# Second layer's edge stage: x1 rows formed in PSUM by identity products, one PSUM buffer for the sums

## The reference

```python
h = relu(layernorm(x))
# first layer: attention messages, summed by dst, then Wo
x = x + h + segment_sum(msg, dst) @ Wo.T + bo          # this is "x1" below
# second layer: weighted graph convolution and a two-layer MLP
h = relu(layernorm(x))
deg = segment_sum([edge_weight, ones], [src, nodes])
norm = rsqrt(deg)[row] * ew * rsqrt(deg)[col]           # edges and self loops
h7 = segment_sum((h @ W)[col] * norm, row) + b          # row = src, col = dst
x = x + relu(h7 @ W1 + b1) @ W2 + b2
```

## Time and profile before

| | |
|---|---|
| time, median of 3 runs | 1871.58 us (1869.59 to 1871.85) |
| the profiled execution | 1868.97 us, of which its span is 1867.3 us |
| busy share of the span | PE 87%, DVE 76%, ACT 60%, POOL 66% |
| first layer's edge stage with what precedes it | from 0 to about 690 us |
| second layer's edge stage | about 690 to 1045 us |
| node stage in full flow | from about 1097 us |

### The profile page before, as it was taken

How to read it: one execution, slowest core, us unless ns; L and a number is a source line. 1 busy time by engine, 2 the same in 40 slices (tenths; PEclk the granted TensorE clock), 3 DMA queues, 4 the chain that set the end, 5 groups by cost and what they waited for, 6 DMA issues and landing times.

```text
span 1867.3 us, 29386 instructions
## 1 busy us (share of the span) xinstructions
PE 1629.1 (87%) x6406; PEld 1099.9 (59%) x6406; DVE 1412.2 (76%) x5503; ACT 1119.3 (60%) x2092; POOL 1227.1 (66%) x864
## 2 busy tenths in 40 slices
PE   8788999999999967676675169999999999999998
PEld 4355666666666635454454046666666666666666
DVE  7986777777777639777776497888888888888873
ACT  0155555556666522222222378889889889989984
POOL 3246777777777646888887765666666666666650
PEclk9999999999999987878777679999999999999999
DMA  9997666666666655555556678999999999999981
GB/s 370 419 415 244 175 175 174 174 174 175 177 177 185 195 136 115 118 111 108 113 115 126 136 200 248 255 266 271 269 268 268 267 270 267 267 268 269 274 230 75
DMA packets 148023, 398.67 MB, mean 214 GB/s; under 512 B 20144, under 2 KB 56756, under 8 KB 147974
## 3 DMA queue, kind: packets, MB, share of 16 engines
q1 hardware_dynamic: 89830, 280.18, 43.8%
q0 software_dynamic: 56416, 115.46, 32.8%
q10 hardware_dynamic: 1728, 2.50, 0.4%
HBM read 217.84 MB, written 180.23 MB: 213 GB/s over the span
## 4 chain that ended last, share of the span: by engine, by line
PE 27%; POOL 25%; issue 13%; DMA 11%; DVE 10%; ACT 7%; another core or an unknown queue 4%; SPq 3%; ACTq 0%; DVEq 0%; POOLq 0%
POOL sums_dram L488 9%; DMA out_dram<-cg 8%; PE bank L1361 6%; PE bank L1350 6%; POOL kept L578 6%; PE bank L1246 4%; POOL cg L492 4%; POOL b_rs L484 4%; ACT z L1054 4%; DVE cg L958 3%; PE bank L1178 2%; PE bank L1253 2%; PE bank L1340 2%; SPq L394 1%
## 5 line engine op out<-in xcount | busy, mean ns | idle before, releaser
L1350 PE MATMUL bank<-kept,w 128*128 128x512 f32 x784 | 355.4, 596 | 0.0
L1361 PE MATMUL bank<-w_sb,kept 128*128 128x256 f32 x1568 | 354.3, 379 | 0.0
L578 POOL TENSOR_TENSOR kept<-kept 128x1024 f32<-128x1024 f32 x98 | 232.4, 2371 | 183.4 <-DVE cg L958 183.4
L1361 PEld LDWEIGHTS bank<-w_sb,kept 128*128 128x128 f32 x1568 | 297.9, 190 | 81.9 <-issue 46.4
L488 POOL DMA_INDIRECT sums_dram<-ub,sidx x148 | 244.1, 1649 | 91.3 <-issue 42.3
L1314 PE MATMUL bank<-cg,en 128*128 128x256 f32 x386 | 132.8, 489 | 124.7 <-issue 80.6
L484 POOL TENSOR_TENSOR b_rs<-b_ve,minus_half 128x8 f32<-128x8 f32 x102 | 210.5, 2064 | 28.7 <-DVE b_ve L975 28.7
L1350 PEld LDWEIGHTS bank<-kept,w 128*128 128x128 f32 x784 | 142.6, 192 | 142.3 <-issue 142.3
L1145 ACT ACTIVATE kept<-kept,b_nb,b_rs 128x256 f32<-128x256 f32 x392 | 202.2, 588 | 21.9 <-DVE b_nb L948 21.9
L1246 PE MATMUL bank<-qkv_w,zT 128*128 128x512 f32 x392 | 192.0, 612 | 21.4 <-DVE msg L815 18.0
L1135 ACT ACTIVATE kept<-kept,b_nb,b_rs 128x256 f32<-128x256 f32 x392 | 202.2, 589 | 12.5 <-DVE b_nb L948 12.5
(11 more groups left out here) (172 smaller groups left out, 3260.3 us busy)
## 6 DMA issues: line engine op xcount, KB each, us to landing
sums_dram<-cg SPq DMA_DIRECT2D x196, 512.0 KB
kept<-in_x_dram SPq DMA_DIRECT2D x97, 512.0 KB, 5.7
kept<-sums_dram POOLq DMA_DIRECT2D x97, 512.0 KB, 9.8
cg<-sums_dram SPq DMA_DIRECT2D x97, 512.0 KB, 8.7
out_dram<-cg SPq DMA_DIRECT2D x97, 512.0 KB, 9.8
row_d<-in_dst_dram SPq DMA_DIRECT2D x49, 128.0 KB
row_k<-keys_dram SPq DMA_DIRECT2D x24, 256.0 KB
row_s<-in_src_dram SPq DMA_DIRECT2D x24, 256.0 KB
```

The costliest lines, as they stand in the source:

```text
L578: pool.tensor_tensor(X1[k.slot(8)], X[k.slot(4)], H[k.slot(2)], ALU.add).then_inc(g_xh, 1)
L1350: ins = pe.matmul(bank[:, 2 + m, :], w01[:, c, m * P:(m + 1) * P], hT[k.slot(2)][:, c * GN:(c + 1) * GN], start=(c == 0), stop=(c == KC - 1))
L1361: ins = pe.matmul(to, rT[k.slot(2)][:, c * GN + j * P:c * GN + (j + 1) * P], w2_sb[:, c, :], start=False, stop=(c == KC - 1), skip_group_c ...
```

## The change

DVE no longer adds `C0` to `kept`. PE gets, between its lookups and its sums, a new step for quad `k = s`: for each pair of chunks an identity product of the two `kept` rows into one PSUM bank, and a second identity product of the gathered rows, accumulated onto it. Four products of 128x512 float32 per quad leave x1 in banks 0 and 1. PE waits for the gathers of quad s and, from the second quad on, for `n_h` of quad s - 1, since there is one such buffer. PE, not DVE, now increments `n_x1`. DVE's statistics and ACT's relus read the banks. The sums use banks 6 and 7 for every quad, and wait for the copy of the quad before rather than of the one before that.

```diff
 # VectorE
-                    dve.wait_ge(n_c0[q], a.turns(2, 16 * Q))
-                    dve.tensor_tensor(quad(kept, a, slice(None)), quad(kept, a, slice(None)), C0[q][:, 0:n, :],
-                                      ALU.add).then_inc(n_x1, 1)
                     dve.wait_ge(n_sel, a.value(1))
                     dve.tensor_tensor(quad(norm, a), quad(found, a), quad(ew_f, a), ALU.mult).then_inc(n_norm, 1)
-                    pass_on(dve, (n_x1, a.value(1)))
+                    dve.wait_ge(n_x1, a.value(1))
                     for i in range(n):
-                        ins = dve.bn_stats(st[q][:, i, :], kept[:, bass.ds(a.value(0, Q) + i, 1), :]
-                                           .rearrange("p a d -> p (a d)"))
+                        ins = dve.bn_stats(st[q][:, i, :], bank[:, i // 2, i % 2 * D:(i % 2 + 1) * D])
 # ScalarE
-                        ins = act.activation(H1e[q][:, i, :], kept[:, bass.ds(a.value(0, Q) + i, 1), :]
-                                             .rearrange("p a d -> p (a d)"), ACT.Relu, bias=nb[q][:, i, :],
-                                             scale=rs[q][:, i, :])
+                        ins = act.activation(H1e[q][:, i, :], bank[:, i // 2, i % 2 * D:(i % 2 + 1) * D], ACT.Relu,
+                                             bias=nb[q][:, i, :], scale=rs[q][:, i, :])
-                        ins = act.activation(UB2[q][i].rearrange("p i d -> p (i d)"), bank[:, 6 * q + i, :], ACT.Copy)
+                        ins = act.activation(UB2[q][i].rearrange("p i d -> p (i d)"), bank[:, 6 + i, :], ACT.Copy)
 # TensorE
+                if k.within(NQ):
+                    n = chunks(k)
+                        pe.wait_ge(n_c0[k.slot(2)], k.turns(2, 16 * Q))
+                    if k.past(1):
+                        pe.wait_ge(n_h, k.value(0))
+                    for i in range(n // 2):
+                        pe.matmul(bank[:, i, :], identity[:, :],
+                                  kept[:, bass.ds(k.value(0, Q) + 2 * i, 2), :].rearrange("p c d -> p (c d)"),
+                                  start=True, stop=False)
+                        ins = pe.matmul(bank[:, i, :], identity[:, :],
+                                        C0[k.slot(2)][:, 2 * i:2 * i + 2, :].rearrange("p c d -> p (c d)"),
+                                        start=False, stop=True)
+                    ins.then_inc(n_x1, 1)
                 if a.within(NQ):
                     q, n = a.slot(2), chunks(a)
                     pe.wait_ge(n_en, a.value(1))
                     pe.wait_ge(n_h, a.value(1))
-                    if a.past(2):
-                        pe.wait_ge(n_UB, a.value(-1))
+                    if a.past(1):
+                        pe.wait_ge(n_UB, a.value(0))
                     for to in range(n):
                         for i in range(to, n):
-                            ins = pe.matmul(bank[:, 6 * q + to // 2, (to % 2) * D:(to % 2 + 1) * D],
+                            ins = pe.matmul(bank[:, 6 + to // 2, (to % 2) * D:(to % 2 + 1) * D],
```

More of the change, by code:

```diff
@@ L880, in messages2 @@
                     ins.then_inc(n_cnt, 1)
-                    if a.reg is None and a.off == NQ - 1:
-                        dve.wait_ge(n_c0[q], 16 * Q * (a.off // 2) + 16 * n)
-                    else:
-                        dve.wait_ge(n_c0[q], a.turns(2, 16 * Q))
-                    dve.tensor_tensor(quad(kept, a, slice(None)), quad(kept, a, slice(None)), C0[q][:, 0:n, :],
-                                      ALU.add).then_inc(n_x1, 1)
                     dve.wait_ge(n_sel, a.value(1))
                     dve.tensor_tensor(quad(norm, a), quad(found, a), quad(ew_f, a), ALU.mult).then_inc(n_norm, 1)
-                    pass_on(dve, (n_x1, a.value(1)))
+                    dve.wait_ge(n_x1, a.value(1))
                     for i in range(n):
-                        ins = dve.bn_stats(st[q][:, i, :], kept[:, bass.ds(a.value(0, Q) + i, 1), :]
-                                           .rearrange("p a d -> p (a d)"))
+                        ins = dve.bn_stats(st[q][:, i, :], bank[:, i // 2, i % 2 * D:(i % 2 + 1) * D])
                     ins.then_inc(n_st, 1)
@@ L1305, in messages2 @@
                     ins.then_inc(n_look, 1)
+                if k.within(NQ):
+                    n = chunks(k)
+                    if k.reg is None and k.off == NQ - 1:
+                        pe.wait_ge(n_c0[k.slot(2)], 16 * Q * (k.off // 2) + 16 * n)
+                    else:
+                        pe.wait_ge(n_c0[k.slot(2)], k.turns(2, 16 * Q))
[9 more added lines that the diff above has]
+                    ins.then_inc(n_x1, 1)
                 if a.within(NQ):
```

## The result

The changed kernel takes 1882.27 us (median of 5 runs, 1878.30 to 1888.31), the kernel before 1871.58 us (5 runs, 1869.59 to 1872.37). The ratio is 1.007 with a 95% interval of 1.0052 to 1.0088: 10.7 us slower. The forecast was 1874, with a range of 1861 to 1891. The profiled execution took 1882.79 us, of which the span is 1881.2; the profiled pair is thus 13.9 us apart in span, the medians 10.7.

A forecast was written before the change was run, and what follows sets the result against it. POOL was taken to bound the edge stage. 20 rounds of 13.7 us against 279.0 give -5.0, start +7.5, tail +0.5, hence +3.0 on 1871.58: 1874.6, rounded to 1874, range 1861 to 1891.

The forecast's parts named there:

- What bounds: Edge stage before the change: POOL itself, with its scatters, gathers and issue gaps, is the bound; no engine releases it.
- 17 us of long scatters: Edge stage, 72 scatters: 129.7 us, against 112.3 at 1.56 each; some 17 of 253 us are standstill, mostly from the add.
- Part 1: Add leaves VectorE: POOL no longer stands still for it; POOL's own round 13.1 us, between 12.9 and 13.9.
- the brush of 0.1 to 0.3 us: POOL's second and third scatters of a round: likely slowed this much by VectorE's counting products, which move toward them.
- Rival 3: Edge rounds: the standstill only moves to the counting products; rounds 14.0 to 14.3 us, time 1879 to 1887; chance 0.16.
- Part 2: x1 on PE: 3.44 us at full clock, fully inside the loop from relus to relus, which becomes 12.9 us.
- Part 3: PE's clock in the edge rounds: a fall costs 1.8 us in full, giving 13.7 us a round; ends 13.1 and 14.9.
- one in three: PE's gaps in the edge rounds: one of three this size lowers the clock, adding 1.8 / 3 to 13.1 us.
- Both rivals of the clock: Edge rounds: clock holds, 12.9 to 13.3 us, chance 0.25; or falls at each gap, 14.5 to 14.9 us, chance 0.13.
- Part 4: Start, tail and rest: first scatter 7.5 us later (5.5 to 9), tail 0.5, the other changes nothing.
- The tail +0.5: Last quads: POOL waits for landings, not PE; the copy of the 24th sums up to 1 us late, so 0.5 us.
- slower, 0.41: Whole kernel: chance 0.41 of slower, against 0.27 faster and 0.32 same, where same is 1867.8 to 1875.3 us.

The follow-up runs named there:

- thin: Kernel before with the add cut to one of each chunk's 256 columns, the rest left out: 1835.3 us, ratio 0.9898.
- split add: Kernel before with the one add of 128x1024 made as four of 128x256 in a row: 1835.7 us, ratio 0.9905.
- with the clock held: Changed kernel with four extra 128x256 products per quad on PE ahead of the lookups: 1849.6 us, 0.998 of the kernel before.
- the later trace: Changed kernel run again unaltered, on chip 1: 1862.9 us, ratio 1.0062 to the kernel before.
- the later traces: Both kernels run again unaltered: the kernel before on chip 12, 1850.9 us; the changed kernel on chip 1, 1862.9 us.

## Why the prediction was right or wrong

**What bounds.** Right for the kernel before. The add's standstill is worth 17 us (the thin and the split add); the prediction's 17 us of long scatters were counted in 18 rounds, while the traces give 12 to 13 us in 20 rounds and 3 to 5 in the start and the tail. In the changed kernel the loop has become the bound over each two rounds (27.5 us against 26.4), though POOL waits in the slow rounds only.

**Part 1.** POOL's own round was put at 13.1 us; it is 13.2 to 13.3. Scatters of 1.71 us beside counting products (867.72) and up to 1.90 us show the brush of 0.1 to 0.3 us. Rival 3, in which the standstill only moves, is refuted: with the clock held the rounds are 13.27 us.

**Part 2.** The loop was put at 12.9 us at full clock and is 12.76. Relus from PSUM take 1.93 us instead of 2.07. That x1 lies fully inside the loop is shown by taking half of it away. What the loop lacked is x1's wait for the gathers, 0.5 us at 867.04.

**Part 3.** The mean round, 13.7, was met by luck, for its two terms were off in opposite directions. Ten rounds of 20 were slow, not one in three. And the loss does not go on top of POOL's round: it goes on top of the loop. In the 20 rounds the loop takes 12.8 us on the mean where the clock held and 14.6 where it fell, and the mean of all is 13.7. The 1.8 us between them are 1.4 to 1.7 of clock, and the rest is x1's wait for the gathers, so the size of a fall was met in sum but not in its parts. Against POOL's 13.2 us a slow round shows only 0.9 us more, because the quick round's 0.45 us to spare, and its own, are used up first. The one in three rested on three gaps. Part 3 also went by the length of the gap, and the runs do not bear that out. Already before the change, gaps of 4.50 and 4.60 us (before 862.20 and 974.85) were followed by first pairs of 0.69 us, at the upper level, and the clock fell only after them. In the later trace two rounds of 16.0 us put the mean at 14.0. Both rivals of the clock are bounded by runs: held, 13.27 us, and the kernel is about 3 us under the one before; down for most of x1, 16.0 us, where 14.9 was my end. That end took 1.8 us a fall from the sums, though Part 2 had x1 itself at up to 6.9 us at half clock.

**Part 4.** The start was put at +7.5 us and is +8.7 in the first result, +7.7 in the later traces. "The tail +0.5" is the step that failed: +7.2 in the first result. I had reasoned that at the tail POOL waits for landings and not for PE. But the change puts x1, which waits for the gathers of quad s, ahead of the sums of s - 1 on PE. The prediction named x1's wait for the relus and not what is queued behind its wait for the gathers: a late landing now delays the scatters of the quad before. The landing was late before the change too (6.75 us of waiting at 1011.49), and no scatter waited for it. Why it is late in some traces and not in others stays open. The copy of the 24th sums, put at up to 1 us late, is 1.8 us late in both traces of the changed kernel (12.5 us from the 23rd quad's scatters instead of 10.7). Where it was not late, on chip 1, the tail was +1.2. The +4.5 us before the edge stage begins are in code that the change does not touch; in the eleven later traces the first gather lies between 670.96 and 676.37 us, so such a step is within the spread of that stage.

**The forecast.** 1874 against 1882.3: the sign that the numbers leaned to (slower, 0.41) came true. The time lies inside the range of 1861 to 1891 but above the 1867 to 1881 that the forecast called its own. 8 us are missing between the medians. Only the profiled pair can be broken down: it is 13.9 us apart, 10.9 more than the 3.0 forecast, of which the tail has 6.7, the stage ahead 4.5 and the start 1.2, less 1.6 of the node stage. In the later traces (chip 12 before, chip 1 after) the start has +7.7, the rounds +1.8 and the tail +1.2. Another 3.0 us lie ahead of the first gather and 0.6 in the node stage, 14.3 us in all; the medians on chip 1 are 10.5 us apart.

## What to carry to other kernels

Before an operation is moved off an engine because it disturbs another, ask how long it must hold what they share: four adds of 256 columns, at 0.2 us more of VectorE's time, gave 17 us, where moving the add to TensorE lost 11. That 17 us is a result on this kernel, in which POOL bounds the stage. An operation that was covered can enter the loop of waits of another engine, in full, with its queue order (what waits behind it) and with TensorE's clock, which a bound elsewhere had made free before. In a loop that is level with the bound, filler work in TensorE's gap can be worth more than it costs: 1.7 us of it a round gave some 13 us.

## What the runs showed that I had not expected

The gap ahead of x1 did not tell whether TensorE's clock would fall. In the first trace it fell after gaps of 1.90 to 2.60 us and held after gaps of 1.90 to 2.99; in the changed kernel's second trace it fell after gaps of 1.89 to 2.97 and held after gaps of 1.89 to 2.13. With extra products ahead of the lookups it held after all gaps of 0.17 to 1.72 us. Once fallen, it cost x1 1.4 to 1.7 us in the slow rounds of the first trace and 2.9 and 3.0 us in the two long rounds of the second. What decides it within gaps of 1.9 to 3 us stays open.

Cutting the add to one column of each chunk (rounds 13.32 us) was no better than cutting it in four (13.26 us).
